# A two-layer mixture-of-experts kernel: rows dispatched by quarters of the tokens, in pages per expert, with the score as a column

## The reference

```python
# layer 0: per-sequence linear map, then a shared FFN and the best of 16 experts
h = einsum(x, c0_w[subject]) + c0_b[subject]
logits = h @ w_router.T; e = argmax(logits)
scores = sigmoid(logits) * one_hot(e)            # one expert per token
gate, up = split((score * h) @ gate_up[e])       # 128 -> 2 x 256
x = x + shared(h) + (up * silu(gate)) @ down[e]
# layer 1: adapter and layer norm per language, then shared FFN and top 2 of 8 experts
h = layernorm(x + relu(x @ W1 + b1) @ W2 + b2) * gamma + beta
combine, dispatch = top2_gating(softmax(h @ router_w), capacity)   # capacity 1280
y = sum over both choices of weight * expert_e(h)   # silu(h @ w1 + b1) @ w2 + b2
x = x + y + 0.1 * shared(h)
```

## Time and profile before

| what | us |
|---|---|
| median of 3 runs | 536.86 (533.89 to 537.79) |
| the profiled execution | 532.79 |
| its span | 531.0 |
| TensorE busy | 447.7 (84% of the span) |
| VectorE busy | 240.2 (45%) |
| ScalarE busy | 247.4 (47%) |
| GpSimd busy | 256.3 (48%) |
| chain that ended last | TensorE 63%, GpSimd 12%, issue 12%, VectorE 5%, DMA 5% |

### The profile page before, as it was taken

How to read it: one execution, slowest core, us unless ns; L and a number is a source line. 1 busy time by engine, 2 the same in 40 slices (tenths; PEclk the granted TensorE clock), 3 DMA queues, 4 the chain that set the end, 5 groups by cost and what they waited for, 6 DMA issues and landing times.

```text
span 531.0 us, 9984 instructions
## 1 busy us (share of the span) xinstructions
PE 447.7 (84%) x3129; PEld 384.3 (72%) x3130; DVE 240.2 (45%) x708; ACT 247.4 (47%) x593; POOL 256.3 (48%) x272
## 2 busy tenths in 40 slices
PE   6798879965999998899997879918999999999900
PEld 4698746644777775477786869908999999999800
DVE  1344486422555554244868865212333233323237
ACT  2234486202555553356456534403555555555424
POOL 3003567771555555500246777760555555655510
PEclk8989999996999999899999799977999999999965
DMA  9999921111322220800001111113234324331169
GB/s 255 398 308 356 393 63 45 55 50 46 78 71 68 78 64 8 237 10 2 11 30 42 45 51 46 55 40 100 66 116 123 107 68 141 109 79 34 35 175 307
DMA packets 66131, 57.96 MB, mean 109 GB/s; under 512 B 9485, under 2 KB 53152, under 8 KB 66099
## 3 DMA queue, kind: packets, MB, share of 16 engines
q1 hardware_dynamic: 58402, 43.99, 27.7%
q0 software_dynamic: 7168, 12.51, 7.3%
q10 hardware_dynamic: 528, 1.05, 0.5%
HBM read 30.28 MB, written 29.47 MB: 113 GB/s over the span
## 4 chain that ended last, share of the span: by engine, by line
PE 63%; POOL 12%; issue 12%; DVE 5%; DMA 5%; ACT 1%; POOLq 1%; SPq 0%; DVEq 0%; ACTq 0%
PE PS L1459 13%; PE PS L1145 8%; POOL rows L568 7%; PE PS L1189 6%; PE PS L1381 4%; POOL rows L536 4%; PE PS L1268 4%; PE PS L1447 4%; PE PS L1448 4%; PE PS L1449 4%; PE PS L1253 2%; PE PS L1255 2%; PE PS L1254 2%; PE PS L1368 2%; PE PS L1206 2%
## 5 line engine op out<-in xcount | busy, mean ns | idle before, releaser
L586 POOL DMA_INDIRECT back<-grp_y,grp_i x80 | 79.6, 996 | 71.9 <-DVE grp_y L1102 58.0
L568 POOL DMA_INDIRECT rows<-disp,slot x64 | 64.9, 1014 | 66.8 <-DVE slot L946 47.2
L1459 PE MATMUL PS<-w2r,act 128*128 128x128 f32 x640 | 77.7, 275 | 0.0
L1459 PEld LDWEIGHTS PS<-w2r,act 128*128 128x128 f32 x640 | 74.7, 191 | 0.0
L735 ACT ACTIVATE act<-PS,b1r 128x256 f32<-128x256 f32 x160 | 62.8, 475 | 14.5 <-PE PS L1449 14.5
L547 POOL DMA_INDIRECT back<-act,blk_i x48 | 47.0, 980 | 42.0 <-DVE act L906 21.3
L1102 DVE TENSOR_TENSOR grp_y<-PS,b2r 128x256 f32<-128x256 f32 x40 | 17.0, 425 | 89.3 <-PE PS L1459 84.4
L596 ACT ACTIVATE xh<-PS 128x256 fp32r<-128x256 f32 (+1 forms) x48 | 20.0, 418 | 74.2 <-PE PS L1145 74.2
L1447 PE MATMUL PS<-xh,w1h 128*128 128x256 f32 x160 | 48.3, 302 | 0.0
L526 POOL TENSOR_TENSOR w_gul<-w_raw,w_guh 128x512 fp32r<-128x512 f32 x16 | 21.0, 1336 | 50.1 <-ACT w_guh L596 50.1
L1448 PE MATMUL PS<-xl,w1h 128*128 128x256 f32 x160 | 44.9, 281 | 0.0
(11 more groups left out here) (216 smaller groups left out, 946.0 us busy)
## 6 DMA issues: line engine op xcount, KB each, us to landing
rows<-zrow SPq DMA_DIRECT2D x32, 258.0 KB, 5.4
grp_x<-rows SPq DMA_DIRECT2D x40, 129.0 KB, 2.3
w_raw<-in_f_gate_up SPq DMA_DIRECT2D x8, 512.0 KB, 7.7
back<-zrow SPq DMA_DIRECT2D x8, 512.0 KB, 6.9
back<-back SPq DMA_DIRECT2D x16, 256.0 KB, 4.6
blk_x<-rows SPq DMA_DIRECT2D x48, 64.5 KB, 1.8
acc<-in_x SPq DMA_DIRECT2D x8, 256.0 KB, 5.2
y0g<-back SPq DMA_DIRECT2D x8, 256.0 KB, 3.2
```

Source lines behind the costliest of these rows:

```text
L568: gp.indirect_dma_start(rows1, bass.IndirectOffsetOnAxis(ap=slot[:, k, t:t + 1], axis=0), disp[:, t, :], None, bounds_check=E1 * CAP - 1, ...
L586: gp.indirect_dma_start(back1, bass.IndirectOffsetOnAxis(ap=grp_i[v % NX][:, u:u + 1], axis=0), grp_y[k][:, u, :], None, bounds_check=last ...
L1459: last = mm(PS[5 + k][:, u * P:(u + 1) * P], act[k][:, c, u * P:(u + 1) * P], w2r[e][:, c, :], start=c == 0, stop=c == C1 - 1)
```

## The change

**Rows** get a second extra column (`ROW = H + 2`): the sigmoid score. The rows are no longer scaled on ScalarE; SiLU takes the score as its scale and VectorE's product multiplies by it (`scalar_tensor_tensor`).

**Layer 0 by quarters.** After each quarter's best expert, the ranks of the quarter (`rank0` on TensorE, in the middle of the next odd turn's matmuls, `read_rank` on VectorE) and its slots (`page_slots`) follow inside the router loop. An expert gets pages of 128 rows as its count grows; a token's slot is its rank plus the start of the old or the new pages. GpSimd scatters a quarter when its slots, scores and rows are there. `page_slots` of a quarter stands on VectorE between the copies of `t` and the copy of the logits of its turn; that of the last quarter stands ahead of the first `glu0`. The block table comes from one comparison of 64 starts with the block's row and a small matmul. The low halves `w_gul` move from GpSimd to VectorE, two behind each `add0`. SyncE writes the zeros of `rows0` ahead of the weights, and now also those of a second array `rows1b`. A block's load waits for the product (`e_ac`) of the block four before, since the product reads the score column.

**Layer 1 by quarters.** The second choice of a quarter is taken from logits minus their maximum, with the first choice masked and a floor of -87 (`second_choices`); first and second choices of a quarter share one running count, one rank matmul pair and one slot computation (`quarter_slots`), one turn later than `first_slots` was. Second choices go to `rows1b`, counted from the end of an expert's range; so the code need not be rewritten, and GpSimd runs through all 64 scatters without waiting for one to land. SyncE loads both arrays for each group of 256 rows, and VectorE merges them (`q_merge`, two operations of 128x129 with a 0/1 column) three groups ahead. Softmax and weights come later, between the steps of the shared FFN.

The core of the diff:

```diff
-    ROW = H + 1
+    ROW = H + 2
@@ SyncE
-            for r in range(0, E1 * CAP, P * 4):
-                sp.dma_start(rows1[r:r + P * 4, :]...
+            for rows in (rows1, rows1b):
+                for r in range(0, E1 * CAP, P * 4):
+                    sp.dma_start(rows[r:r + P * 4, :]...
@@ load_block
-                    sp.wait_ge(e_xt, j - 3)
-                    sp.wait_ge(e_ix, j - 3)
+                    sp.wait_ge(e_ac, j - 3)
@@ load_group
                 sp.dma_start(grp_x[k][:, :, :], at(rows1_q, m)).then_inc(gx_ld[k], 16)
+                sp.dma_start(grp_z[k][:, :, :], at(rows1b_q, m)).then_inc(gx_ld[k], 16)
@@ GpSimd
-            for e in range(E0):
...
-                gp.tensor_tensor(w_gul[:, cols], w_raw[:, cols], w_guh[:, cols].bitcast(fp32),
-                                 ALU.subtract).then_inc(g_lo, 1)
             for t in range(NT):
-                if t % (NT // 2) == 0:
-                    pool.wait_ge(slots0, t // (NT // 2) + 1)
-                if t % G == 0:
-                    pool.wait_ge(scaled, t + G)
+                if t % RT == 0:
+                    pool.wait_ge(slots0, t // RT + 1)
+                    pool.wait_ge(scored, t // RT + 1)
+                    pool.wait_ge(tok_done, (t + RT) // G)
...
-                    if (k, t) in ((0, NT - 8), (1, HT - 8)):
-                        h = k
-                        pool.wait_ge(sc1[0][h], 16 * HT)
...
+            for r in range(NR):
+                pool.wait_ge(slots1, r + 1)
+                pool.wait_ge(b_tk, (r + 1) * RT // G)
+                for k, rows in ((0, rows1), (1, rows1b)):
+                    for t in range(r * RT, (r + 1) * RT):
+                        gp.indirect_dma_start(rows, ...slot[:, k, t:t + 1]..., disp[:, t, :], ...)
@@ ScalarE
-                for t in range(n * 2 * G, min((n + 1) * 2 * G, NT)):
-                    sc.activation(disp[:, t, 0:H], disp[:, t, 0:H], ACT.Copy,
-                                  scale=score[:, t:t + 1]).then_inc(scaled, 1)
-                sc.activation(blk_s[k][:, :], PS[k][:, 0:F0], ACT.Silu).then_inc(e_sl, 1)
+                sc.activation(blk_s[k][:, :], PS[k][:, 0:F0], ACT.Silu,
+                              scale=blk_x[s][:, H + 1:H + 2]).then_inc(e_sl, 1)
@@ VectorE, layer 0 router loop
             for n in range(NG + 1):
...
+                if n >= 3 and n % 2 == 1:
+                    read_rank((n - 3) // 2)
                 if n < NG:
                     for b in range(2, 4):
...
+                if n >= 3 and n % 2 == 1:
+                    page_slots((n - 3) // 2)
...
+            def page_slots(r):
...
+                    link(v.tensor_tensor(et(older, RT), et(rank, RT), bc(held.unsqueeze(2), over), ALU.is_lt))
+                    link(v.tensor_tensor(et(older, RT), et(older, RT), bc(gap.unsqueeze(2), over), ALU.mult))
+                    link(v.tensor_tensor(rank, rank, older, ALU.add))
+                link(v.tensor_tensor(et(rank, RT), et(rank, RT), bc(at_new.unsqueeze(2), over), ALU.add))
+                link(v.tensor_tensor(rank, rank, mask[:, r * KQ:(r + 1) * KQ], ALU.mult))
+                link(v.tensor_reduce(slotF[:, 0, r * RT:(r + 1) * RT], by_t(rank, RT), AX.X, ALU.add))
+                v.tensor_copy(slot[:, 0, r * RT:(r + 1) * RT], ...).then_inc(slots0, 1)
@@ VectorE, shared FFN of layer 0
+            read_rank(NR - 1)
+            page_slots(NR - 1)
             glu0(0)
...
             for n in range(1, NG + 1):
                 if n < NG:
                     glu0(n)
                 add0(n - 1)
+                for e in (2 * n - 2, 2 * n - 1):
+                    low_half(e)
@@ VectorE, layer 1 router loop
-                if (n - 3) * G % RT == 0 and n > 3:
-                    first_slots((n - 3) * G // RT - 1)
+                if n >= 6 and n % 2 == 0:
+                    quarter_slots((n - 6) // 2)
...
+                if n >= 5 and n % 2 == 1:
+                    second_choices((n - 5) // 2)
@@ VectorE, experts
+            def q_merge(q, k, turn):
+                dve.wait_ge(gx_ld[k], turn * 32 + 32)
+                for u in range(U):
+                    ins = v.scalar_tensor_tensor(out=grp_x[k][:, u, 0:H + 1], in0=grp_z[k][:, u, 0:H + 1],
+                                                 scalar=at_q(secondQ, q)[:, u:u + 1], in1=grp_x[k][:, u, 0:H + 1],
+                                                 op0=ALU.mult, op1=ALU.add)
+                ins.then_inc(q_mg, 1)
@@ TensorE
                     for b in range(QB):
+                        if b == 2 and n >= 3 and n % 2 == 1:
+                            rank0((n - 3) // 2)
...
-                        if i == 2 and (n - 3) * G % RT == 0 and n > 3:
-                            rank1((n - 3) * G // RT - 1)
+                        if i == 2 and n >= 6 and n % 2 == 0:
+                            rank1((n - 6) // 2)
```

More of the change, by code:

```diff
@@ L136, in adaln_moe_two_layers @@
         grp_x = [sb(f"grp_x{k}", [P, U, ROW]) for k in range(NX)]
+        grp_z = [sb(f"grp_z{k}", [P, U, ROW]) for k in range(NX)]
         grp_y = [sb(f"grp_y{k}", [P, U, H]) for k in range(2)]
@@ L223, in adaln_moe_two_layers @@
         ones_f = sb("ones_f", [P, E0])
-        jrow = sb("jrow", [1, NBLKP])
-        cmpj = act0[0:1, 0:NBLKP * (E0 - 1)].rearrange("o (j e) -> o j e", e=E0 - 1)
-        bexp = sb("bexp", [1, NBLKP])
+        assert E0 * RT == KQ and 2 * E0 * NR + 8 * E0 + 2 * KQ == W
+        startE = t2[:, 0:NR * E0]
+        stepE = t2[:, NR * E0:2 * NR * E0]
+        page = [t2[:, 2 * NR * E0 + k * E0:2 * NR * E0 + (k + 1) * E0] for k in range(8)]
+        rank = t2[:, 2 * NR * E0 + 8 * E0:2 * NR * E0 + 8 * E0 + KQ]
+        older = t2[:, 2 * NR * E0 + 8 * E0 + KQ:W]
+        blkF = sb("blkF", [P, 1])
+        bexpF = sb("bexpF", [P, 1])
         w_at = sb("w_at", [1, NBLKP + 2, 2], i32)
@@ L274, in adaln_moe_two_layers @@
         blocks0 = sem("blocks0")
-        scaled = sem("scaled")
-        sc0 = sem("sc0")
+        scored = sem("scored")
+        sc0 = [sem(f"sc0_{k}") for k in range(2)]
+        rk0 = sem("rk0")
+        bx_rows = sem("bx_rows")
+        pe_bx = sem("pe_bx")
         pe_gu = sem("pe_gu")
@@ L456, in _ @@
             for k in range(TOP_K):
-                for h in range(2):
-                    sp.wait_ge(sc1[k][h], 16 * (NT // 2))
+                sp.wait_ge(sc1[k], 16 * NT)
             for m in range(NX):
@@ L803, in _, with own, first_expert @@
             by_t = lambda a, n: a.rearrange("p (e i) -> p i e", i=n)
+            def own(a, r):
+                return et(a[:, r * KQ:(r + 1) * KQ], RT)
+            def first_expert(r):
+                first_max(lg, E0, t1, own(mask, r).rearrange("p e i -> p i e"), r * RT, RT)
+                v.engine_nop().then_inc(mx0, 1)
+                both = slice(r * KQ, (r + 1) * KQ)
+                link(v.tensor_tensor_scan(seen[:, both], rst1[:, :], mask[:, both], 0.0, ALU.mult, ALU.add))
+                v.engine_nop().then_inc(mk0, 1)
@@ L949, in first_choices, with quarter @@
[L949 to L962 removed]
+            def quarter(r):
+                return slice(r * RT * E1, (r + 1) * RT * E1)
@@ new lines, in chosen, with first_choices, second_choices @@
+            def chosen(a, r, k):
+                return et(a[:, r * KQ + k * E1 * RT:r * KQ + (k + 1) * E1 * RT], RT)
+            def first_choices(r):
+                first_max(lg, E1, t2, chosen(mask, r, 0).rearrange("p e i -> p i e"), r * RT, RT)
+            def second_choices(r):
+                cols = quarter(r)
+                one, two = (chosen(mask, r, k).rearrange("p e i -> p i e") for k in range(TOP_K))
+                link(v.tensor_tensor(te(t1[:, cols], E1), te(lg[:, cols], E1),
+                                     bc(m1[:, r * RT:(r + 1) * RT].unsqueeze(2), [P, RT, E1]), ALU.subtract))
+                link(v.scalar_tensor_tensor(out=te(t2[:, cols], E1), in0=one, scalar=-BIG, in1=te(t1[:, cols], E1),
+                                            op0=ALU.mult, op1=ALU.add))
+                link(v.tensor_scalar(t2[:, cols], t2[:, cols], FLOOR, None, ALU.max))
+                first_max(t2, E1, t1, two, r * RT, RT)
+                both = slice(r * KQ, (r + 1) * KQ)
+                link(v.tensor_tensor_scan(seen[:, both], rst1[:, :], mask[:, both], 0.0, ALU.mult, ALU.add))
+                v.engine_nop().then_inc(mk1, 1)
@@ L1115, in _ @@
             split_weights(0, 16, 0)
+            for q in range(3):
+                q_merge(q, q, 0)
             q_index(0, 0)
```

383 lines of the change are left out of this document (213 added, 170 removed).

## The result

| | before | after |
|---|---|---|
| median of four runs each | 535.4 us | 542.4 us (541.1 to 542.8) |
| after / before | | 1.021, 95% interval 1.011 to 1.030 |
| span of the profiled execution | 531.0 | 540.7 |
| TensorE / VectorE / ScalarE / GpSimd busy | 447.7 / 240.2 / 247.4 / 256.3 | 457.8 / 288.7 / 242.9 / 235.3 |
| moved by DMA | 58.0 MB | 68.9 MB |

The change makes the kernel about 2% slower. Forecast were 540 us and a span of 534.2. The span is 6.5 us longer than that: 4.9 of it in layer 0, up to the last scatter of a block, and 1.6 in layer 1.

The account below looks back on a forecast made before the run. TensorE paces layer 1's expert loop; two earlier places end on GpSimd's scatters. Terms 3.7 + 3.3 + 2.9 - 6.6 + 0.5 - 0.5 - 0.1 = +3.2 us give span 534.2, 536.0 and, by the median, 540; range 531 to 547.

Parts of the forecast that it names:

- Last features late: Layer 0 router end: quarter 2's bookkeeping on VectorE delays the last copy of features that TensorE waits for, +3.7 us.
- Quarter 3 ahead of the first product: Layer 0, shared FFN start: rank matmuls and quarter 3's slots stand before the first product, +3.3 us.
- The clock: Layer 0: TensorE's two new gaps make the granted clock fall to half, +2.9 us, bounds 0 and 4.5.
- Wait before the first block: Layer 0, before the blocks: the wait for scatters goes and the gap becomes 2.3 us instead of 8.86, -6.6 us.
- Quarters 0 and 1: Layer 0 router: their bookkeeping falls beside matmuls of the next group and costs nothing, 1 us as upper end.
- Block loads: Layer 0 block loop: loads waiting for the product just fit; few slow landings cost +0.5 us, bounds 0 and 6.6.
- the better clock: Layer 0 block loop: it starts at a better clock than after 8.86 us idle, -0.5 us.
- Layer 1: Layer 1 before its expert loop: later first scatter, unbroken scatters, second load and merge together give -0.1 us.
- Expert loop: Layer 1 expert loop: VectorE's added 0.7 us per group of 3.43 costs nothing.
- Rival A: Layer 0, faster: bookkeeping finds room and the two gaps do not open, +9.9 falls away, 530 us; chance 0.15.
- B: Layer 0 blocks, slower: loads come late, 6.6 us in all, total +9.8, 546.7 us; chance 0.18.
- C: Layer 1, slower: VectorE's added operations hold scatters through the shared port, last scatter 6 us later, 545 us; chance 0.07.

Follow-up runs that it names:

- e2: e1 with the third quarter's slots also behind the first two products and the last quarter's split behind groups 1 and 2: 530.35 us, ratio 0.993 to the kernel before.
- e1: Changed kernel with the first two shared FFN products ahead of the last quarter's slots on VectorE: 532.7 us, ratio 0.997 to the kernel before.
- e3: Changed kernel with unused matmuls on zeros filling TensorE's two gaps, VectorE's order untouched: 535.3 us, ratio 1.002 to the kernel before.
- b0: The kernel before, unchanged, run once more for a second profile, on a chip where engines stood idle: 596.7 us.
- e4: Changed kernel with the 16 low halves spread over VectorE's turns 1 to 6 instead of two per turn: 538.4 us, ratio 1.013 to the kernel before.
- b2: b1 with the block table's small matmul and its two conversions one turn later: 526.2 us, ratio 0.983 to the kernel before.
- b1: e2 with ScalarE's last roundings and scores behind the SiLUs and the low halves spread: 605.3 and 599.1 us on slow chips, ratio 1.007 in the second.

## Why the prediction was right, and where it was not

The mechanism held: the gain ahead of the blocks is given back by bookkeeping in VectorE's order. The time (542.4, forecast 540, range 531 to 547) held partly by luck. The sum said +3.2 us; by spans the change cost 9.7, by medians 7.0. The forecast came so near because it added 4.1 us, by which the profiled execution of the kernel before lay under its median, to the sum; that of the changed kernel lay at its median (542.42), and a fourth run lowered the median before from 536.86 to 535.38. By the steps of the sum:

- **Last features late, +3.7**: +3.4. Eighteen operations in 4.5 us (68.11 to 72.60), reckoned at 4.7: the shift, priced at 0.47 by a row that began while GpSimd subtracted, took 0.17. e2 takes the wait away.
- **Quarter 3 ahead of the first product, +3.3**: +2.9. e1 takes it away.
- **The clock, +2.9, bounds 0 and 4.5**: +5.7 by the table, 5.3 by e3, above the upper bound. This term was mis-sized most. I took the price of one fall from the subject matmuls of the earlier trace rows, 5.34 us instead of 3.68, and did not look at how long the clock was at half there. It was so for 3.4 of the 5.34 us (26.34 to 29.76), and half of that is the 1.7. Behind each new wait it was at half for 5.5 to 5.9 us of work, which costs 2.7 to 3.0. The kind of matmul matters little: 14 subject matmuls in 2.80 us at half against 32 in 3.50 at full, and 1.71 us against 0.86 for a pair of 128x512. The fall at the first block was not foreseen. Windows of the kernel before, then of the changed kernel:

```profile
26.40:29.60 3.20, 3.20 (x17) 2.65 (x16) 0.00 (x0) 0.69 (x2) 0.00 (x0) 0.50 1.06 372
29.80:31.30 1.50, 1.50 (x15) 1.35 (x13) 0.68 (x1) 0.29 (x1) 0.00 (x0) 1.00 1.09 297
```
```profile
21.20:24.00 2.80, 2.80 (x14) 2.33 (x14) 0.00 (x0) 0.59 (x1) 0.00 (x0) 0.50 1.07 342
28.70:32.20 3.50, 3.50 (x32) 3.33 (x32) 1.37 (x2) 1.41 (x3) 0.00 (x0) 1.00 1.05 389
```

- **Wait before the first block, -6.6**: -6.6. 2.29 us as forecast.
- **Quarters 0 and 1, nothing, at most 1**: no wait for VectorE, but the router stage is 2.6 us longer. The step that failed is that I counted only VectorE's side. TensorE's three rank matmuls stand in the middle of the subject matmuls: 38.56 - 34.58 = 3.98 us in such a turn against 3.61, three times, 1.1 us. Another 0.7 is a later start of the first subject matmul (10.26 against 9.58; 9.95 to 11.02 in all variants, 9.50 in b0), and the rest lies in waits that the profile puts down to "issue", in front of the subject matmuls (7.9 us against 7.3). Neither was traced to a cause. Up to 3.5 us more come and go between variants with the same code there (66.6 to 70.8). For e4, the 70.8, it is the clock: at half for 13.6 us of that stage against 6.8 in the changed kernel, which costs 3.4.
- **Block loads, +0.5, and the better clock, -0.5**: +0.45 together. The step between blocks is the same 1.48; each stall at the loop's head, once in eight blocks, is 1.12 to 1.17 instead of 1.02 to 1.11. Landings had a median of 1.9, against 1.8 in the sum. The clock over the first 8 us of blocks was 0.79 against 0.72 before, worth half a us as forecast. SiLU with a scale column took 473 ns (475 by the row with a bias column), the product 484 instead of 425.
- **Layer 1, -0.1**: from the last block's scatter to the first transposition of a group, 150.91 before and 150.90 after. Its parts held: first scatter +9.45 (9.3), 63 steps in 82.55 (82.6), the second load and merge +1.3. That it is exact to 0.1 is partly luck: with the same code in layer 1 the stretch was 150.6 us in b2 and 148.3 to 149.1 in e1 to e4. Around 225 us the clock of the changed kernel fell for 3.4 us, as before's did around 217 and b2's around 208; in e1 to e4 it did not fall there.
- **Expert loop, nothing**: +0.4, and **the rest** +1.1, not foreseen. It was 28.5 to 28.9 us in all six undisturbed profiles of the changed kernel and its variants and 27.8 in the one of before. The transfers that read the results back land later in it (5.69 us against 4.82 in the chain of waits); no run here shows why.
- **Rival A** (no gaps) fell for this kernel. Its price was -6.7 us against the kernel before. e2, which comes near to its case but keeps a wait of 1.93, measured -3.4 by the medians (533.7 to 530.35), b2 -8.0. **B** fell, by the step of 1.48. **C** fell: a scatter came every 82.55 / 63 = 1.31 us against 1.30, 0.6 us in all and not 6, though VectorE was busy in 7.6 to 9.3 of each 12 us from 280 to 352. The port rule of the Trainium skill ("SBUF — State Buffer", section "SBUF: two separate sides") did not show as a cost on GpSimd's scatters here. With the subtraction off GpSimd, the 128x128 comparison of the earlier trace rows took 0.29 instead of 0.97, which agrees with the rule.

## What to carry over

When work is split to start an engine earlier, put its bookkeeping behind, not ahead of, the operation that the pacing engine waits for, and only as much per turn as the turn has room for: the changed kernel was 2% slower than the kernel before with its bookkeeping in front, and 1.7% faster with it and some of ScalarE's work behind. An idle time of the matmul engine is to be priced at its length plus the half clock behind it. For that, read in the windows how long the clock stayed at half, and not only how long one row took. A forecast of a difference should be checked as a difference: an offset added to it can hide that the sum is a third of what came. Removing one wait uncovers the next (VectorE's, ScalarE's, the table's), so read the timelines of all engines at the place again after every step.

## What the runs showed of the hardware

- Granted clock: idle times of 4.20 and 5.48 us of TensorE each led to 6.8 us at half clock, 5.5 to 5.9 of it over work. After 2.29 us the clock fell for 6.8 us (e2), for 3.4 us (changed kernel, e3) or not at all (e1). After 1.93 us (e2) and 0.78 us (e4, b2) it did not fall. Matmuls on zeros in the two long idle times kept it at 1.00 (e3).
- Half clock doubles dense 128x512 matmuls (0.86 to 1.71 us a pair), and the 128*32 subject matmuls nearly so (109 to 200 ns each, by 32 in 3.50 us and 14 in 2.80). A row of 5.34 us that looks like a factor of 1.45 was at half for only 3.4 us of its length.
- A scale operand from a column cost ScalarE's SiLU 473 - 384 = 89 ns at 128x256; the Trainium skill ("ScalarE: Activation LUTs", section "What ACT_TABLE_LOAD costs") gives about 93 for such an operand, and the trace agrees.
- The same kernel took 534 us on some chips and 591 to 603 on others, where engines stood still for up to 34 us at a time; a version that was 1.7% faster on the former gained nothing in its nearly identical form (b1) on the latter.
